# Writing the causal mask of all-diagonal score units with ScalarE before the scores, in a two-layer transformer kernel

## The reference

```python
qkv = (xn @ qkv_w + qkv_b).reshape(b, s, 3, H, HD)
q, k, v = ...
scores = jnp.einsum('bhqd,bhkd->bhqk', q, k) / np.sqrt(HD).astype(np.float32)
causal = jnp.triu(jnp.ones((s, s), dtype=bool), 1)
scores = jnp.where(causal[None, None], -jnp.inf, scores)
attn_w = jax.nn.softmax(scores, axis=-1)
attn = jnp.einsum('bhqk,bhkd->bhqd', attn_w, v)
```

## Time and profile before

| | us |
|---|---|
| median of 3 runs (lowest, highest) | 1511.62 (1510.42, 1512.54) |
| the profiled execution | 1513.78 |
| its span in the profile | 1512.0 |
| TensorE busy in the span | 1366.1 (90%) |
| VectorE busy | 1251.6 (83%) |
| ScalarE busy | 1079.6 (71%) |
| GpSimd busy | 278.4 (18%) |

### The profile page before, as it was taken

How to read it: one execution, slowest core, us unless ns; L and a number is a source line. 1 busy time by engine, 2 the same in 40 slices (tenths; PEclk the granted TensorE clock), 3 DMA queues, 4 the chain that set the end, 5 groups by cost and what they waited for, 6 DMA issues and landing times.

```text
span 1512.0 us, 31977 instructions
## 1 busy us (share of the span) xinstructions
PE 1366.1 (90%) x13016; PEld 565.2 (37%) x13016; DVE 1251.6 (83%) x1715; ACT 1079.6 (71%) x1239; POOL 278.4 (18%) x624
## 2 busy tenths in 40 slices
PE   6699999999998768888679999999999999999886
PEld 3334434444443235456323332332333333323455
DVE  8988888888884386985899999999999999997043
ACT  6167777777777567763358888888888888888652
POOL 5022313222222151431100000000000000001252
PEclk9689999999999989999889999999999999999998
DMA  5510111101000000021110000000000000000001
GB/s 179 169 44 24 39 31 31 40 24 46 24 4 2 1 1 0 1 81 67 42 64 24 23 24 23 24 21 14 16 23 24 23 23 24 3 3 3 1 15 42
DMA packets 38995, 47.90 MB, mean 32 GB/s; under 512 B 11072, under 2 KB 20160, under 8 KB 38720
## 3 DMA queue, kind: packets, MB, share of 16 engines
q1 hardware_dynamic: 38416, 45.31, 9.8%
q10 hardware_dynamic: 432, 0.53, 0.1%
HBM read 30.22 MB, written 15.47 MB: 30 GB/s over the span
## 4 chain that ended last, share of the span: by engine, by line
PE 73%; DVE 11%; ACT 7%; issue 5%; POOL 3%; DMA 1%; ACTq 0%; POOLq 0%; SPq 0%; DVEq 0%
PE ps L428 29%; PE ps L406 15%; PE ps L385 12%; PE ps L554 7%; DVE l_negp L326 3%; PE ps L445 3%; ACT l_outT L304 2%; ACT shared L298 2%; POOL n_rs L516 2%; PE ps L391 2%; DVE n_bst L497 1%; PE ps L547 1%; PE ps L1042 1%; PE ps L910 1%; PE ps L562 1%
## 5 line engine op out<-in xcount | busy, mean ns | idle before, releaser
L326 DVE TENSOR_REDUCE l_negp<-ps 128x2 f32<-128x1024 f32 (+2 forms) x832 | 956.4, 1181 | 57.7 <-PE ps L391 33.3
L298 ACT ACTIVATE shared<-ps 128x1024 f32<-128x1024 f32 (+1 forms) x832 | 820.5, 991 | 185.3 <-PE ps L406 155.7
L428 PE MATMUL ps<-shared,l_vs 128*32 128x256 f32 (+3 forms) x6648 | 515.4, 385 | 18.9 <-ACT l_outT L304 14.1
L385 PE MATMUL ps<-Ks,Qs 48*128 48x512 bf16 (+3 forms) x1792 | 329.2, 368 | 31.1 <-DVE l_negp L326 22.0
L406 PE MATMUL ps<-Qs,Ks 51*128 51x512 bf16 (+3 forms) x1792 | 321.1, 367 | 14.5 <-ACT shared L298 6.3
L428 PEld LDWEIGHTS ps<-shared,l_vs 128*32 128x32 f32 x6648 | 136.6, 108 | 198.0 <-issue 163.4
L406 PEld LDWEIGHTS ps<-Qs,Ks 51*128 51x128 bf16 x1792 | 81.1, 93 | 316.8 <-issue 181.3
L385 PEld LDWEIGHTS ps<-Ks,Qs 48*128 48x128 bf16 x1792 | 87.5, 94 | 171.8 <-ACT shared L298 96.0
L282 POOL TENSOR_SCALAR_AFFINE_SELECT shared<-shared 128x512 f32<-128x512 f32 x128 | 81.7, 640 | 311.1 <-ACT shared L298 309.0
L267 POOL CAST l_parts<-l_negm 128x16 bf16<-128x16 f32 x64 | 12.6, 197 | 442.3 <-DVE l_negm L331 439.2
L391 PE MATMUL ps<-mask,id 64*128 64x128 bf16 x1024 | 68.5, 222 | 0.0
(11 more groups left out here) (160 smaller groups left out, 1094.7 us busy)
## 6 DMA issues: line engine op xcount, KB each, us to landing
Qs<-scr_q SPq DMA_DIRECT2D x128, 64.0 KB
Ks<-scr_k SPq DMA_DIRECT2D x64, 96.0 KB
Qs<-scr_q SPq DMA_DIRECT2D x128, 32.0 KB
Ks<-scr_k SPq DMA_DIRECT2D x64, 64.0 KB
scr_q<-own SPq DMA_DIRECT2D x4, 768.0 KB, 3.6
scr_q<-shared SPq DMA_DIRECT2D x4, 768.0 KB, 3.5
scr_k<-own SPq DMA_DIRECT2D x4, 768.0 KB, 4.9
scr_k<-shared SPq DMA_DIRECT2D x4, 768.0 KB, 4.8
```

What stands on the lines that cost most here:

```text
L298: act.activation(dst, src, ACT.Exp, scale=SCALE).then_inc(exped, 1)
L326: dve.tensor_reduce(dst, src, AX_X, ALU.max, negate=True).then_inc(reduced, 1)
L385: last = pe.matmul(outs[par], Qs[s][r:r + MROW, h2, qt * P:(qt + 1) * P], Ks[s][r:r + MROW, h2, at:at + w], start=True, stop=True)
L428: last = pe.matmul(pv_ps[32 * h:32 * h + 32, a:a + wide], vs[g % 2][:, kt, h, :], pT[m % PRING][:, h, a:a + wide], start=m == u.first_step ...
```

## The change

The units whose keys are all diagonal (`w == P` and `at == qt * P`) get a number in `preset`, 32 units in all. For each of them a new entry "preset" stands in the order at the max unit's tick, ahead of the key unit of that tick. On ScalarE it waits for the bank (`slot_free`, now usable by either engine) and copies the mask tile `mask_neg` (128 x 128, bf16), read four times over, into the unit's part of the two banks: 512 elements per partition. On TensorE the unit waits for this copy instead of the bank, its four score matmuls add to what stands there (`start=False`), and its mask matmuls are left out. The other units with a diagonal are as before.

```diff
+        self.preset = {}
+        for i, (_, _, _, qt, _, at, w, causal) in enumerate(self.max_unit):
+            if causal and w == P and at == qt * P:
+                self.preset[i] = len(self.preset)
...
             out += [(i, ("key", i)), (i - ahead, ("max", i))]
+            if i in self.preset:
+                out.append((i - ahead, ("preset", i)))
...
-        kinds = ("split", "key", "max", "weigh", "evacuate", "turn_max", "turn_out")
+        kinds = ("split", "preset", "key", "max", "weigh", "evacuate", "turn_max", "turn_out")
...
     def scalar(act, entry):
-        if entry[0] == "key":
+        if entry[0] == "preset":
+
+            unit = ("max", entry[1])
+            if u.preset[entry[1]] == 0:
+                act.wait_ge(masks_in, 2)
+            slot_free(act, unit)
+            dst = slot(unit)[:, :, 0:PAIRS * P].rearrange("p two (h k) -> p two h k", h=PAIRS)
+            src = mask_neg[:, :].unsqueeze(1).unsqueeze(1).to_broadcast([P, 2, PAIRS, P])
+            act.activation(dst, src, ACT.Copy).then_inc(preset, 1)
+        elif entry[0] == "key":
...
-            slot_free(pe, entry)
+            cut = causal and at + w == (qt + 1) * P
+            if entry[1] in u.preset:
+                pe.wait_ge(preset, u.preset[entry[1]] + 1)
+            else:
+                slot_free(pe, entry)
...
                     last = pe.matmul(outs[par], Qs[s][r:r + MROW, h2, qt * P:(qt + 1) * P],
-                                     Ks[s][r:r + MROW, h2, at:at + w], start=True, stop=True)
-                if causal and at + w == (qt + 1) * P:
+                                     Ks[s][r:r + MROW, h2, at:at + w], start=entry[1] not in u.preset, stop=True,
+                                     skip_group_check=entry[1] in u.preset)
+                if cut and entry[1] not in u.preset:
```

More of the change, by code:

```diff
@@ L167, in order, with attention @@
                     (self.k_ends[q] + 2, ("evacuate", q)), (self.k_ends[q] + 4, ("turn_out", q))]
-        kinds = ("split", "key", "max", "weigh", "evacuate", "turn_max", "turn_out")
+        kinds = ("split", "preset", "key", "max", "weigh", "evacuate", "turn_max", "turn_out")
         return [(t - start, e) for t, e in sorted(out, key=lambda x: (x[0], kinds.index(x[1][0]), x[1][1:]))]
-def attention(nc, ctx, all_units, place, scr, scr_m, slots, loaded, handed, v_tm, attn_tm, ident, mask2, id2, ident_bf,
-              halved, pT, ps):
+def attention(nc, ctx, all_units, place, scr, scr_m, slots, loaded, handed, v_tm, attn_tm, ident, mask2, id2, mask_neg,
+              ident_bf, masks_in, halved, pT, ps):
     PRING, MCOLS = 4, GH * CT
@@ L199, in attention @@
     max_rows = [sem(f"max_rows{i}") for i in range(4)]
-    (scored, reduced, masked, evacuated, out_turned, recips, max_split, split_part,
+    (scored, preset, reduced, masked, evacuated, out_turned, recips, max_split, split_part,
      max_turned, max_copied, max_stored, v_clear, v_ready, cleared, joined) = (sem(n) for n in (
-         "scored reduced masked evacuated out_turned recips max_split split_part "
+         "scored preset reduced masked evacuated out_turned recips max_split split_part "
          "max_turned max_copied max_stored v_clear v_ready cleared joined").split())
@@ L283, in gpsimd, with slot_free @@
                                    pattern=[[0, GH], [1, P]], channel_multiplier=-1).then_inc(masked, 1)
-    def scalar(act, entry):
-        if entry[0] == "key":
+    def slot_free(eng, entry):
+        if place.before[entry] is None:
+            return
+        kind, i = place.before[entry]
+        if kind == "max":
+            eng.wait_ge(reduced, i + 1)
+        elif kind == "key":
+            eng.wait_ge(exped, i + 1)
+        elif kind == "turn_max":
+            eng.wait_ge(max_copied, i + 1)
+        elif kind == "turn_out":
+            eng.wait_ge(normed, i + 1)
+        elif kind == "first":
+            eng.wait_ge(handed.v_made[0], i + 1)
+        elif kind == "mid":
+            eng.wait_ge(handed.v_made[1], i + 1)
+        else:
+            eng.wait_ge(handed.out_made, i + 1)
+    def scalar(act, entry):
+        if entry[0] == "preset":
[7 more added lines that the diff above has]
+        elif entry[0] == "key":
             g, m, pairs = u.key_unit[entry[1]]
@@ L349, in vector @@
                 .then_inc(normed, 1)
[L351 to L369, removed]
     def tensor(pe, entry):
@@ L1181, in two_layer_kernel @@
             nc, ctx, units, program, (scr[0:2], scr[2:4]), scr_m, slots, loaded, handed, v_tm, attn_tm, ident[:, :],
-            mask2, id2, ident_bf[:, :], halved, pT, ps)
+            mask2, id2, mask_neg, ident_bf[:, :], cut_out, halved, pT, ps)
         def free_for(of):
```

## The result

| | before | after |
|---|---|---|
| median of 5 runs, taken side by side (us) | 1512.54 | 1522.07 |
| lowest, highest | 1510.42, 1515.65 | 1521.42, 1523.12 |
| the profiled execution, its span | 1513.78, 1512.0 | 1522.01, 1520.3 |

The ratio is 1.005, 95% interval 1.003 to 1.0071, that is 4.5 to 10.7 us: the kernel is slower, by 9.5 us between the medians. The forecast was 9.4 us, 1521.0 in a range of 1513.5 to 1526.0.

The account below looks back on a forecast made before the run. TensorE, 96% busy, was taken to bound the first attention. Copy waits less saved masks cost 0.41 us at qt = 0 and 0.26 at qt = 4, 14 times each: 9.4 us over 1511.62, 1521.0, range 1513.5 to 1526.

Parts of the forecast that it names:

- The bound and the path: First attention: TensorE, 96% busy, bounds it; the changed units lie on its in-order chain, so delays pass through in full.
- The masks, 0.22 us a unit: Max pass, units qt = 0 and qt = 4: dropping 8 mask matmuls takes 0.22 us off TensorE per unit.
- The copy, 0.59 us: ScalarE: each of the 32 added copies of 512 elements takes 0.59 us; up to 0.09 more allowed for its operand.
- The copy doesn't overlap its predecessor: ScalarE: the copy starts 0.04 us after the exponential ahead ends; with overlap the sum would be 5.5 us, not 9.4.
- qt = 0, +0.41: Units qt = 0: first load 0.63 us later, unit 0.22 shorter, so the weigh step comes 0.41 us later.
- qt = 4, +0.26: Units qt = 4: first matmul at 237.93 instead of 237.45, 0.48 us later, less 0.22 of masks: 0.26 us.
- 14 of each, and zero at the start: 14 units of each kind pay in full; the other four, before 84 us, are taken as zero.
- The sum, 9.4 us: Whole kernel: 14 x (0.41 + 0.26) = 9.4 us slower, 1521.0 us on the median; chance 0.75.
- The backlog of the next exponential adds nothing: ScalarE at qt = 0: the next exponential, pushed to about 254.0, is absorbed by 0.58 us of idle time.
- The hidden copy: Rival: the copy is done before TensorE reaches the unit, saving 28 x 0.22 = 6.2 us, 1505.4; chance 0.06.
- The absorbed delay: Rival: the copy overlaps and qt = 4's shift is taken up further on; 2.8 us remain, 1514.4; chance 0.15.
- The clock did not fall: Rival: added waits lower TensorE's clock; about 2 us for a later rise, up to 26 for one period; chance 0.04.

Follow-up runs that it names:

- the halves: The change made for units qt = 0 only, or for qt = 4 only: +6.9 us (1.0044) and +3.8 us (1.0023) against the kernel before.
- the masks alone: The change without its copies: the 32 units lose their masks and nothing is written in their place; -5.7 us (0.9959) against the kernel before.
- copies aside: The kernel before plus the 32 ScalarE copies, written to an SBUF tile nobody reads, all masks kept: +1.3 us (1.0012) against the kernel before.
- unit behind the weigh step: The change with its 32 max units half a tick later, after TensorE's weigh step: +3.2 us (1.002) against the kernel before.

## Why the prediction was right, step by step

- **The bound and the path.** Right. TensorE's steps in order set the period, the two units lie on them, and what each loses or saves goes through: the halves add up to the whole, and the masks alone save their full 0.46. The copies take 0.60 us, the periods are 26.83 us, and 768 mask matmuls are left, where 0.59, 26.9 and 768 were forecast.
- **The masks, 0.22 us a unit.** 0.23 measured.
- **The copy, 0.59 us.** 0.60 in 31 of 32, 0.58 in the first. The extra 0.09 us allowed for its operand was not needed: a bf16 tile read four times over, into PSUM, takes 8 ns more than L339's read of 512 elements from PSUM into SBUF (593).
- **The copy doesn't overlap its predecessor.** Shown: it starts 0.03 us behind the exponential's end at both kinds of unit, and 0.03 to 0.04 at all 28. This was the choice between 9.4 and 5.5 us. In the same rows the exponential behind the copy, which does not depend on it, starts 0.06 us before the copy's recorded end (124.28 against 124.34). The Trainium skill (ScalarE: Activation LUTs, What ACT_TABLE_LOAD costs) gives an overlap of about 93 ns for activations back to back; the trace agrees for the pair without a dependence, roughly, and not for the pair in which the second waits for the first one's signal.
- **qt = 0, +0.41.** 0.41 between the units, 0.40 in the period of the kernel with this unit alone.
- **qt = 4, +0.26.** 0.23. (The recorded steps add up to a matmul at 237.92, not 237.93.) The copy started 0.03 us behind the exponential, not 0.04, and TensorE's first matmul 0.05 behind the copy, not 0.08. The period is therefore 26.83 and not 26.87.
- **14 of each, and zero at the start.** 14 periods, each 0.633 us longer, make 8.9 us, where I had 9.4. In the profile after, the first load of qt = 0 comes at 97.62, 1.21 later than before, of which the unit's own wait is 0.63. Of the other 0.58, 0.34 is there ahead of the first copy: ScalarE's last conversion before it starts at 44.14, 43.80 before. Until 82 us, behind all four early copies, it is 0.40 (an exponential at 82.78, 82.38 before), so these four, less their masks, cost 0.06 us at most, as good as the zero I had put. The last 0.18 comes between 82 and 88 us, where the clock rises later: the mean granted clock from 84 to 88 us is 0.86, and 0.96 before. No run tells whether the change moves that rise. The start differs between kernels by far more (the first copy of the sums comes between 84.79 and 91.02 us).
- **The sum, 9.4 us.** What the trace settles is the 8.9 us of the periods. Near its end the first attention is 9.46 us late in the profile after (a copy of the sums at 483.55, 474.09 before), ScalarE's table load ahead of the second attention 11.08 (781.55 and 770.47), the last copy of the sums 8.86 (1436.03 and 1427.17) and the whole span 8.3: stages that the change doesn't touch differ by as much as 2 us between two executions. That the medians differ by 9.5, 0.1 from the forecast, is luck beyond what their interval of 4.5 to 10.7 us can tell.
- **The backlog of the next exponential adds nothing.** Right for the sum, but for a reason given only by halves. It is hidden because TensorE, held by the copy, is late by itself. Where TensorE does not wait for the copy at qt = 0 (copies aside, unit behind the weigh step), the backlog shows: that part of the period is 0.15 and 0.09 us longer than before.
- **The rivals.** The hidden copy is out: TensorE waited for 30 of 32. The absorbed delay is out: all of 0.63 shows in every period up to the last. The clock did not fall in the attention: it is 1.00 from 100 to 440 us, as before, with waits of 0.67 us at qt = 0 and 0.29 at qt = 4 added; longer ones weren't tried. In the stretch from 72 to 84 us it is at the same level as before:

```profile
72.00:84.00 12.00, 10.83 (x71) 3.22 (x73) 9.09 (x10) 7.08 (x9) 3.68 (x9) 0.50 0.24 70
```

## What to carry to other kernels

Work moved off the engine that bounds, onto one whose result it then waits for, trades occupancy for latency: here 0.23 us of matmuls for 0.64 us of copy, wait and hand-over at the one unit and 0.45 at the other, though the receiving engine stood idle a quarter of the time. Whether an idle share is of use is read at the place: what ran directly ahead of the new instruction, and what the waiting engine has left to do meanwhile. Giving the waiting engine other work returns most of the loss but then meets the next thing in order (here ScalarE's backlog, then VectorE's queue), so here the gain lay in leaving work out rather than in moving it.

## What the runs showed of the hardware beyond that

ScalarE's copy of the same 512 elements took 601 ns into PSUM and 631 ns into SBUF, in 31 of 32 each. The row of the copy in the kernel with the copies aside:

```profile
L323 ACT ACTIVATE l_aside<-mask_neg x32: 614/631/631, 44.8 to 448.0; 128x512 f32<-128x512 bf16 x32
```

The Trainium skill (ScalarE: Activation LUTs, Step-by-step: what each stage is for) says that an activation into PSUM is faster than one into SBUF; the 30 ns agree. TensorE's answer to ScalarE also had two sizes. At qt = 0 the first load comes 0.11 us behind the copy's end, at qt = 4 the first matmul 0.05 behind it; in the kernel before it was 0.12 and 0.05 behind an exponential. The slower of the two waits for two semaphores there, the copy's and the loads', but no run took one of them away, so the cause stays open. The copies aside point the same way: with a second semaphore to wait for, they start 0.08 to 0.10 us behind the exponential's end, where the copies of the change start 0.03 to 0.04 behind it; but they also write elsewhere.
